# A fused patch-embedding, attention and mixture-of-experts kernel: the 16 left-over tokens' expert work moved from block 1 into tiles 5 to 11, image 2 moved behind tile 1's first gate, and identity matmuls added

## What is computed

```python
h = concat([patches @ proj_w.T + proj_b, txt], axis=1)          # [16, 113, 192]
h = h + attention(layernorm(h))                                  # 12 heads, diagonal masked from token 1 on
x = layernorm(h)
pe = softmax(posembed @ pos_w + pos_b, axis=-1)                  # [16 experts, 192]
y = (silu(x @ sg_w) * (x @ su_w)) @ sd_w                         # shared MLP, 384 wide
for i in range(16):
    gate = x * pe[i] @ gate_w + gate_b                           # [1808, 192]
    weight, idx = top_k(gate, 96)
    xg = take_along_axis(x, idx, axis=-1) * softmax(weight)
    y = y + (silu(xg @ eg_w[i]) * (xg @ eu_w[i])) @ ed_w[i]
out = h + (silu(layernorm_gb(y) @ m1_w + m1_b) @ m2_w + m2_b)
```

## Time and profile before

| | |
|---|---|
| median of 3 runs | 2601.3 us |
| profiled execution, its own time | 2600.56 us |
| its span, first to last instruction | 2598.7 us |
| DVE busy | 2503.0 us, 96% |
| PE busy | 2292.9 us, 88% |
| POOL busy | 1790.0 us, 69% |
| ACT busy | 1701.1 us, 65% |
[...]

### The profile page before, as it was taken

How to read it: one execution, slowest core, us unless ns; L and a number is a source line. 1 busy time by engine, 2 the same in 40 slices (tenths; PEclk the granted TensorE clock), 3 DMA queues, 4 the chain that set the end, 5 groups by cost and what they waited for, 6 DMA issues and landing times.

```text
span 2598.7 us, 48229 instructions
## 1 busy us (share of the span) xinstructions
PE 2292.9 (88%) x11466; PEld 1248.8 (48%) x11466; DVE 2503.0 (96%) x13317; ACT 1701.1 (65%) x4088; POOL 1790.0 (69%) x2163
## 2 busy tenths in 40 slices
PE   7788989899999889889888998888889988889888
PEld 4555445455454454444544444444445444344344
DVE  5897999999999999999999999999999999999994
ACT  4355676766676667677766767667576676666664
POOL 1245777777686777777777777767677677676674
PEclk7688899989899899999899899899997998978789
DMA  4021122222221222222222222222222122222221
GB/s 109 16 57 28 47 56 61 46 50 55 52 56 50 48 58 46 57 48 53 54 53 54 52 52 51 49 59 47 58 46 54 45 55 52 53 47 53 45 51 34
DMA packets 124863, 133.58 MB, mean 51 GB/s; under 512 B 40019, under 2 KB 112734, under 8 KB 124582
## 3 DMA queue, kind: packets, MB, share of 16 engines
q1 hardware_dynamic: 123270, 128.02, 21.1%
q0 software_dynamic: 880, 1.62, 0.2%
q10 hardware_dynamic: 432, 0.86, 0.1%
HBM read 102.58 MB, written 27.87 MB: 50 GB/s over the span
## 4 chain that ended last, share of the span: by engine, by line
DVE 82%; PE 10%; ACT 2%; DMA 2%; issue 2%; POOL 1%; SPq 0%; DVEq 0%; ACTq 0%; POOLq 0%
DVE idx L665 29%; DVE keys L667 28%; DVE vals L661 24%; PE ps L1306 2%; PE ps L1387 1%; DMA rows<-digit_d 1%; DVE digits L634 1%; PE ps L1363 1%; DVE nmax L603 1%; DMA digit_d<-dcode 1%; PE ps L1294 1%; PE ps L1319 1%; PE ps L1360 1%; PE ps L1268 1%; DMA looked_s<-in_mask_in 1%
## 5 line engine op out<-in xcount | busy, mean ns | idle before, releaser
L1136 POOL TENSOR_TENSOR picked<-looked_s,code 128x384 f32<-128x384 f32 (+1 forms) x896 | 879.4, 990 | 459.5 <-ACT looked_s L862 458.1
L665 DVE FIND_INDEX8 idx<-vals,keys 128x8 uint16<-128x192 f32 x2712 | 944.2, 349 | 0.0
L862 ACT ACTIVATE looked_s<-ps 128x384 f32<-128x384 f32 (+1 forms) x896 | 440.3, 491 | 658.6 <-PE ps L1306 656.0
L667 DVE MATCH_REPLACE8 keys<-vals,keys 128x192 f32<-128x192 f32 x2486 | 844.0, 339 | 0.0
L1306 PE MATMUL ps<-code,table 128*128 128x384 f32 (+1 forms) x1824 | 843.5, 546 | 0.0
L661 DVE MAX8 vals<-keys 128x8 f32<-128x192 f32 x2712 | 822.7, 343 | 17.7 <-ACT keys L811 17.7
L852 ACT ACTIVATE code<-ps 128x768 f32<-128x768 f32 (+1 forms) x896 | 725.5, 810 | 66.0 <-PE ps L1294 52.2
L1294 PE MATMUL ps<-rows,codew 17*128 17x384 bf16 (+1 forms) x1824 | 320.9, 348 | 177.8 <-ACT code L852 110.2
L1294 PEld LDWEIGHTS ps<-rows,codew 17*128 17x128 bf16 x1824 | 86.9, 92 | 737.2 <-ACT code L852 371.4
L1306 PEld LDWEIGHTS ps<-code,table 128*128 128x128 f32 x1824 | 317.4, 206 | 188.9 <-issue 152.4
L1363 PE MATMUL ps<-xwt,wexp 96*96 96x128 f32 x1792 | 271.8, 299 | 34.9 <-ACT xwt L818 32.7
(11 more groups left out here) (170 smaller groups left out, 2235.6 us busy)
## 6 DMA issues: line engine op xcount, KB each, us to landing
wexp<-in_w_exp SPq DMA_DIRECT2D x58, 576.0 KB, 4.3
wdown<-in_w_down SPq DMA_DIRECT2D x58, 576.0 KB, 4.5
digit_d<-dcode SPq DMA_DIRECT2D x56, 384.0 KB, 2.6
rows<-digit_d SPq DMA_DIRECT2D x220, 96.0 KB
table<-norm_d SPq DMA_DIRECT2D x448, 3.0 KB
patch<-in_patches SPq DMA_DIRECT2D x16, 108.0 KB, 4.8
norm_d<-hs SPq DMA_DIRECT2D x16, 84.8 KB
tok_d<-h SPq DMA_DIRECT2D x16, 84.8 KB
```

The lines of the kernel that those rows point to most:

```text
L665: found = nc.vector.max_index(idx[:, par, e, at], vals[:, par, e, at], from_keys[:, e, :])
L667: nc.vector.match_replace(from_keys[:, e, :], vals[:, par, e, at], from_keys[:, e, :], NEG).then_inc(chain, 1)
L862: nc.scalar.activation(looked_s[:, o % 4, 0:w], ps[:, LOOK_B[o % 2], 0:w], ACT.Copy).then_inc(looked_out, 1)
L1136: nc.gpsimd.tensor_tensor(picked[:, o % PICKS, w], looked_s[:, o % 4, w], code[:, o % 4, 1, w], ALU.mult).then_inc(picked_ready, 1)
```

## The change

It has three parts, and some smaller moves with them.

1. **Rides.** The left-over tokens' units leave slot 1. The bands become four quarters (4 experts each), placed in slots of tiles 5, 6, 7 and 9, each in the tile and group whose weights are in SBUF then, and the two shared units in tiles 10 and 11. Each writes its sum to the shared bank `MISC_B`; ACT copies it to `y_rest`, and the next adds it again by one identity matmul. The final stage of the left-over tokens stands in slot (12, 3). The two loads in slot 1 go, and the head loads experts 0 to 7 instead of 8 to 15.
2. **Image 2.** In `FIRST`, image 2's stages stand behind image 1's `turn_h` and block 1's first gate, image 0's `turn_x`, `q`, `k`, `v` ahead of image 1's `embed`, and `gate_rest` one stage later. Image 2's maxima move on DVE from round 4 to round 9 of block 1, image 3's from block 3 to block 5; image 1's first maximum is taken ahead of block 0's rounds. Image 1's `rinv` is a DVE reciprocal in block 0's round 5 instead of a POOL power.
3. **Identity products.** `keep_warm` multiplies the identity by itself into a bank that nobody reads, at 20 places of the head (50 products), once in slot 55 and before the last stages. An ACT copy of one element stands ahead of the first embedding, and the attention mask is loaded ahead of image 1's patches.

```diff
+DOWN_LAG = 4
+REST_SPOTS = {(5, 0, 13): (0, "quarter", 0), (6, 2, 1): (1, "quarter", 1), (7, 3, 1): (2, "quarter", 2), (9, 0, 13): (3, "quarter", 3),
+              (10, 2, 1): (4, None, 0), (11, 2, 1): (5, None, 1)}
+RIDES = [(5, 0), (6, 1), (7, 2), (8, 3)]
...
+        if i < AHEAD:
+            step = 3 - GAP[REST_OF[0]] + 1
...
-    spots = {(0, 0, 2): 1, (1, 0, 4): 2}
+    spots = {(0, 0, 0): (1, 1), (0, 0, 1): (1, 2), (1, 0, 9): (2, None)}
     for i in range(AHEAD, IMAGES):
         rounds = 2 * ROUNDS * (ATT_PE[i, "s2"] + 5 - 8) // OCT + 2 * (2 * ROUNDS)
-        block, r = divmod(rounds, 2 * ROUNDS)
-        spots[block, r // ROUNDS, r % ROUNDS] = i
+        block, r = divmod(rounds + (ROUNDS if i == AHEAD else 0), 2 * ROUNDS)
+        spots[block, r // ROUNDS, r % ROUNDS] = i, None
...
-REST_LIST = [(0, "band", 1), (1, None, 0), (2, None, 1), (3, "band", 0)]
...
+WARM_AHEAD = {(0, "embed"): 5, (0, "turn_x"): 1, (1, "turn_x"): 1, (1, "q"): 2, (0, "mix"): 3, (0, "turn_o"): 2, (0, "proj"): 1,
+              (0, "turn_h"): 1, (1, "s0"): 3, (1, "t0"): 1, (1, "t1"): 1, (1, "t2"): 1, (1, "mix"): 2, (1, "turn_o"): 4,
+              (1, "proj"): 1, (1, "turn_h"): 9, (2, "turn_x"): 1, (2, "s0"): 3}
+WARM_POS, WARM_PACKING, WARM_LAST, WARM_TURN, WARM_UP, WARM_FINAL = 6, 2, 9, 5, 2, (9, 3, 5)
...
-                    if (t, g) == (1, 0):
-                        load_experts(0, 0, 1)
-                        load_experts(GRP, 1, 1)
-                    elif t and (t, g) != (1, 1):
-                        load_experts(GRP * g, g % 2, units_before(t if g >= 2 else t - 1) + 2 + GRP * ((g + 2) % 4 + 1))
+                    if t and (t, g) not in ((1, 0), (1, 1)):
+                        load_experts(GRP * g, g % 2, last_unit(t if g >= 2 else t - 1, (g + 2) % BPT))
...
+                            if (n, pair, r) == (0, 0, 5):
+                                dve.wait_ge(misc_out, stage_out(1, "mix"))
+                                nc.vector.reciprocal(rinv[:], mix[:, :, DH]).then_inc(att_rinv, 1)
...
+                nc.scalar.activation(nmax[0:1, 0:1], ones[0:1, 0:1], ACT.Copy)
                 for i, stage in FIRST:
...
+                def keep_warm(times, bank):
+                    for _ in range(times):
+                        nc.tensor.matmul(ps[:, bank, 256:384], ident[:], ident[:], start=True, stop=True)
...
+                    if rest_tile:
+                        pe.wait_ge(misc_out, MISC_NTH["rest", u] - 1)
+                        if u:
+                            pe.wait_ge(misc_out, MISC_NTH["rest", u - 1])
+                            nc.tensor.matmul(ps[0:REST, MISC_B, 0:D], ident[0:REST, 0:REST], y_rest[:], start=True, stop=False)
...
+                        if n == LAST - 1 and o == PREPARE:
+                            pe.wait_ge(misc_out, MISC_NTH["turn", n - 1])
+                            keep_warm(WARM_LAST, MISC_B)
```

More of the change, by code:

```diff
@@ L99 @@
 ATT_MORE[AHEAD - 1, "proj"] = ATT_PE[AHEAD - 1, "proj"] + 2
+for _c in range(3):
+    ATT_MORE[AHEAD - 1, f"s{_c}"] = _c
 for _i in range(AHEAD, IMAGES):
@@ L155 @@
 TURN = 3
-DOWN_LAG = 4
 PREPARE, PREPARE_LAST = 8, 12
@@ L173, in unit_steps @@
         if tm == 0:
-            units = REST_LIST
+            continue
         for (u, e, half), spot in zip(units, TAIL_SPOTS if n > LAST else UNIT_SPOTS[g]):
             at[OCT * n + spot] = (tm, u, e, half)
+    for (t, g, o), (u, e, half) in REST_SPOTS.items():
+        assert OCT * block_no(t, g) + o not in at
+        at[OCT * block_no(t, g) + o] = (0, u, e, half)
     return at
@@ L189, in gate_steps, with final_steps @@
     return at
-def final_steps(offsets):
-    return {OCT * block_no(t + 1, 1) + o: (t, what) for t in range(TILES + 1) for o, what in offsets.items()}
+def final_steps(offsets, rest):
+    at = {OCT * block_no(t + 1, 1) + o: (t, what) for t in range(1, TILES + 1) for o, what in offsets.items()}
+    at.update({OCT * block_no(*REST_SLOT) + o: (0, what) for o, what in rest.items()})
+    return at
 UNIT_AT = unit_steps()
@@ L224, in slots, with last_unit, rest_resid_slot @@
             slot(t, g)
-def units_before(t):
-    return 0 if t == 0 else REST_UNITS + UNITS * (t - 1)
+def last_unit(t, m):
+    own = [UNIT_NTH[t, 2 + GRP * m + GRP - 1]]
+    return max(own + [UNIT_NTH[0, q] for q in range(QUARTERS) if RIDES[q] == (t, m)])
+def rest_resid_slot(t, g):
+    return (t, g) == (REST_SLOT[0], REST_SLOT[1] - 1)
 def pairs_before(t, g):
@@ L597, in _, with score_max @@
                 nc.vector.tensor_scalar(pe_row, pe_row, pstat[:, 2:3], None, ALU.mult).then_inc(pe_norm, 1)
-                def score_max(i):
-                    for c in range(HG):
+                def score_max(i, only=None):
+                    for c in range(HG) if only is None else [only]:
                         dve.wait_ge(misc_out, stage_out(i, f"s{c}"))
@@ L1338, in up @@
                             pe.wait_ge(nt_mlp_in, 16 * tm)
-                    if e == "band":
+                    if e == "quarter":
                         pe.wait_ge(misc_out, MISC_NTH["turn", 0])
-                        for par in range(2):
-                            pe.wait_ge(weights_in[par], 32 if u == 0 else 64)
+                        pe.wait_ge(weights_in[half % 2], 32 * expert_load(*RIDES[half]) + 32)
                     elif e is not None and (e % GRP == 0):
@@ L1356, in up @@
                                                            (nt_rest if rest_tile else nt_mlp)[:, k, :], start=(k == 0), stop=(k == 1))
[L1357 to L1361 removed]
+                            elif e == "quarter":
+                                for x in range(GRP):
+                                    own = slice(GRP * REST * (half % 2) + x * REST, GRP * REST * (half % 2) + (x + 1) * REST)
+                                    ins = nc.tensor.matmul(dst[:, x * REST:(x + 1) * REST], wexp[:, half % 2, x, at:at + HALF],
+                                                           xwt_rest[:, half // 2, own], start=True, stop=True)
                             else:
@@ L1465, in _ @@
                         gate(1, 0, 0)
-                    if (i, stage) == (2, "s2"):
-                        for g, pair in ((0, 1), (1, 0), (1, 1)):
-                            gate(1, g, pair)
+                    if (i, stage) == (2, "embed"):
+                        gate(1, 0, 1)
+                        gate(1, 1, 0)
+                    if (i, stage) == (2, "turn_x"):
+                        gate(1, 1, 1)
                 pe.wait_ge(placed_w, 5 + PER // 2)
```

216 lines of the change are left out of this document (128 added, 88 removed), and 6 rows, old and new, of the table FIRST.

## The result

The changed kernel takes 2593.4 us (median of 20 executions, 2577.1 to 2608.7) against 2600.5 of the kernel before (20, 2594.8 to 2608.3). The ratio is 0.9966, 95% interval 0.9952 to 0.9979: a little faster, by 7 us where 33 were forecast, and outside the range of 2558 to 2580. The profiled one had 2582.1 us of its own, so its trace is one of a better execution. One execution of `e5_no_warm`, at 2622.1 us, was a slow one and is left out of that kernel's median.

A forecast was written before the change was run, and what follows sets the result against it. DVE, busy 2503.0 of 2598.7 us, was taken as the bound, so only its idle time could be gained. The four terms, -4.5 - 9.0 - 19.2 - 0.5 = -33.2 us, took the median 2601.3 to 2568, range 2558 to 2580.

The forecast's parts named there:

- Term 1: Head, DVE's first keys: earlier by 4.5 us, between -9 and 0, from new order and held PE clock.
- Term 2: Head, from block 0's keys to block 1's on DVE: 32.0 us become 23.0, -9.0 (range -9.0 to -7.4).
- Term 3: DVE's waits for scores of images 3 and 4: 19.7 us become 0.5, -19.2; remaining wait bounded by 0 and 7.
- a wait at image 4: Body of DVE: a wait showing at images 2, 4, 9 or 12 would mean the prediction is wrong.
- cost nothing, under cover: Slots with rides: a quarter's 6.2 us of PE is hidden by the 9.0 us between scores and maxima.
- Rival D: Rides' lag passes 9.0 us and DVE waits at the maxima; at worst 2612, slower; chance 0.04.
- Term 4: Tail behind DVE's last block, where PE sets the pace: -0.5 us, between -4 and +3.
- C: New image wait: image 2's scores late, or image 3's maxima hold ACT and image 4 waits; ten us, 2578; chance 0.09.
- Rival E: Change fails: slot 1 as long, first keys unmoved, only the gain between blocks 0 and 1, -8: 2593; chance 0.03.

The follow-up runs named there:

- e5_no_warm: Changed kernel without any of its identity products: 2601.1 us, ratio 0.9997 to the kernel before.
- e2_no_hold: Changed kernel with image 3's maxima 12 rounds earlier on DVE: 2581.9 us, ratio 0.9920 to the kernel before.
- e7_light_no_hold: Changed kernel with image 3's maxima 12 rounds earlier and quarters doing one octet's rows per expert group in place of four: 2568.0 us, ratio 0.9879.
- e8_double: Changed kernel with the quarters' `up` products made twice, into the same places: 2612.1 us, ratio 1.0049 to the kernel before.
- e10_places: Changed kernel with image 3's maxima 12 rounds earlier, gates earlier from tile 3 on, quarters 0 and 1 moved to later slots: 2570.8 us, ratio 0.9897.
- e11_before_gates: Control: the kernel before the change with each tile's gates made earlier, nothing else: 2598.5 us, ratio 0.9998.

## Why the prediction was wrong

**Term 1, -4.5: right.** 50.78 became 46.24 in one trace; in the other trace of the same program it was 49.26, and in the nine traces of edited kernels that keep the products 46.4 to 47.4. Without the products it was 49.93, so the early table load and the new order bring at most about 0.9 (PE had 0.67 there from 34.8 to 50.3 us, before 0.50) and the clock the rest, when it is held (0.89 from 34 to 80 us in the one execution, 0.81 in the other). Of the 4.5 us forecast, 3.5 were the clock's: some 8 of the 11.81 us in which PE is busy from 34.8 to 50.3 at 0.50, times 1 - 2.14 / 3.79 from the embedding's twelve matmuls at two places. The granted clock over those was 1.00 at the second place and 0.55 on average at the first. The 8 us were an estimate that no run shows. What the runs showed is 1.00 from 34.8 to 50.3 in the first trace of the changed kernel, `gate_rest` in 1.47 us there in place of 2.90 (2.83 without the products), and the first keys 3.69 us ahead of those without the products, in the second trace 0.67.

**Term 2, -9.0: right.** 23.04 us from the first keys to block 1 (23.0 forecast), 23.7 in the second trace, and no wait for keys.

**Term 3, -19.2: the waits of image 3 went as said, but their sum did not.** "I leave 0.5 us of wait" was 6.95 at image 4 in the first trace and 8.30 in the second; a wait at image 4 was one of the signs that the prediction had named for being wrong. The step that failed is that ACT's hold for the maxima would be "up to 10 us" and leave 4 of image 4's 14 us in hand. It was 15.18, and the lag of slots 4 to 6 was 36, 43 and 43 us, some 20 more than without it (20, 23 and 23 in `e2_no_hold`), so that tile 3's first keys came late too (2.72, 9.35). Taking it away gave 11.5 us. I had the hold from the diff and could have sized it: image 3's exponentials stand in slot 3's steps 5 to 7, and the maxima behind round 3 of block 5 (counted from 0), both known numbers.

**The rides: "cost nothing, under cover" was the main error.** Three quarters of their work cost 16.8 us by the kernel with light rides, and their `up` doubled 18.7 more. The prediction had that price itself: 6.2 us for a quarter if nothing covers it, which is 18.6 for three quarters of four. Rival D's statement that the rides reach DVE was right, though mostly at keys and not at maxima, but I gave it a chance of 0.04 for two reasons that fell:
- The cover of 9.0 us was measured at one kind of meeting point, the scores. The other, a tile's first keys, I never looked at. In the trace of before they came 3.6 us ahead at tile 6, and at tile 12 DVE already waited 0.22 for them.
- The cover was measured with DVE where it stood before. Terms 1 to 3 bring DVE forward by some 26 us at that point, and the engines behind it had no 26 us to give: PE was busy 448.83 of 500 us. I counted 4.4 us a block as free, and the doubled rides show no such cover; that it is so because PE, ACT and POOL hand each other every step is my reading. The gain and the cover were the same microseconds, and I spent them twice.

**Term 4, -0.5:** -1.0 in the first trace (59.0 against 60.0), +1.1 in the second. Right within what the executions differ by.

**The sum.** With hold and most of the rides' work gone, the kernel takes 2568.0. That this is the forecast to the microsecond is luck: it is the median of four executions from 2565 to 2578, and in its trace the head gained 11.9 us and not 13.5, the waits 19.7 and not 19.2, and the tail 1.7 and not 0.5. Within that, head, units out of slot 1 and tail were sized rightly, and the two items set at 0.5 and 0 were not: the hold 8.7 to 11.5 and the rides 13.9 to 16.8, by which is taken away first, 25.4 together (2593.4 - 2568.0). I had treated C and D as rivals, each alone; both were there at once and partly. Rival E names the very time that came out, 2593, but that too is luck: the first keys did come earlier and slot 1 took 46 us, before 69.

**Shown and open.** Shown by undoing: the hold and the rides. Shown by doubling: more work in the rides is not covered. Shown by the control: the early gates are worth something only where keys are late. That keys had no time left because DVE came earlier is read from traces (3.6 us in hand before, none in `e7_light_no_hold`); rides in the kernel before, with DVE where it stood, were not run, so what they would cost there isn't known. Only associated: that an execution's clock sets how much it loses, with the exception named above. Why quarter 2 meets the lower level in one execution and not in another stays open, and so does what lowers the clock at quarter 0 each time; slot 17 had 0.79 on average before the change too, with no ride in it.

## What to carry to other kernels

A change that takes waits away from the engine that sets the time moves it forward against all the others: list every kind of point where it meets them, take the slack of each in the trace of before, and subtract the forecast gain before anything is costed as covered. Where the slack is then gone, added work reaches the time (here 16 to 19 us more of PE became 18.7), and so does a wait that the followers have for that engine (ACT's 15.18 us cost 8.7 to 11.5). The cheap cure here was to make early what is needed first (gates, loads), which was worth nothing that could be told before the change and 12.8 us after it. And a unit of work cost by the clock that it met: a quarter's `up` took 2.89 us at 0.99 and 5.30 at 0.50, so look up the granted clock of the place before work is moved there.

## What the runs showed of the hardware

The 32 small matmuls of a quarter's `up` took 2.89 us at a granted clock of 0.99 and 5.30 at 0.50, at the same place of the same program in two executions. In the first trace quarter 0 ran wholly at the lower level (5.30) and quarter 3 in part (3.54, at 0.78). The wait for image 11's last scores was 5.80 us, to the hundredth, in five traces (the changed one's second trace, `e2_no_hold`, `e5_no_warm`, `e8_double`, `e10_places`), as it was for image 3's before. I read it so: when the group of scores ahead was late already, DVE waits the followers' step to the next one, not a length that grows with the lag.

One DVE instruction of a block, the digits (`L678`), took from 0.24 to 2.60 us in the first trace. The longest on DVE, and what POOL did meanwhile:

```profile
2348.18 2.60 DVE L678 TENSOR_SCALAR digits<-idx 128x384 uint16<-128x384 uint16 x1
```

```profile
2348.03 0.72 POOL L1141 TENSOR_TENSOR hid<-prod_s,turned_s 96x256 f32<-96x256 f32 x1
2348.71 1.95 POOL L1205 TENSOR_TENSOR picked<-looked_s,code 128x384 f32<-128x384 f32 x2
```

POOL's three instructions end at 2350.66 and the digits at 2350.78. At 1135.07, when POOL ran nothing, the same instruction took 0.24. All 22 in this trace that took over 0.4 us end 0.11 to 0.12 us behind the end of an instruction of POOL, so I take what is over 0.24 for a wait for POOL, which no view of waits shows. Why DVE waits there isn't shown. In the rows above it did not get in between POOL's instructions, which stood back to back for 2.63 us. The group of 57 took 21.7 (`e11_before_gates`) to 35.5 us in the 14 traces, 32.1 before the change. At 0.24 each it would be 14, so I estimate that 8 to 22 us of what I called DVE's own time is this wait. That is as large as the effects that the experiments measure, and a trace has to be read with that in mind.
